# Causal mask of an attention's diagonal tile: a matmul with a mask, or an add on VectorE

## What is computed

```python
q = rotary_embedding(q, seq_len, HEAD_DIM)
k = rotary_embedding(k, seq_len, HEAD_DIM)
scores = jnp.einsum('bqhd,bkhd->bhqk', q, k) * scale
mask = jnp.tril(jnp.ones((seq_len, seq_len), dtype=bool))[None, None, :, :]
scores = jnp.where(mask, scores, NEG_INF)
weights = jax.nn.softmax(scores, axis=-1)
out = jnp.einsum('bhqk,bkhd->bqhd', weights, v)
```

## Time and profile before

| what | value |
|---|---|
| median of three runs | 2990.51 us |
| lowest, highest | 2986.48, 2994.03 us |
| profiled execution | 2990.0 us, of which 2988.3 us are the span of the program |
| busy share of the span: PE, DVE, ACT, POOL | 91%, 66%, 56%, 50% |
| granted TensorE clock, mean | 0.965 |

### The profile page before, as it was taken

How to read it: one execution, slowest core, us unless ns; L and a number is a source line. 1 busy time by engine, 2 the same in 40 slices (tenths; PEclk the granted TensorE clock), 3 DMA queues, 4 the chain that set the end, 5 groups by cost and what they waited for, 6 DMA issues and landing times. The chain is left out here.

```text
span 2988.3 us, 49627 instructions
## 1 busy us (share of the span) xinstructions
PE 2731.2 (91%) x15887; PEld 2292.6 (77%) x15887; DVE 1978.7 (66%) x3727; ACT 1663.8 (56%) x3193; POOL 1491.8 (50%) x1681
## 2 busy tenths in 40 slices
PE   5899989999989999899999689999959999999997
PEld 3788868888868888788888568778747888888886
DVE  5476766666756766566766669888845666666665
ACT  2456565656556656556666533333316676666665
POOL 1567555666646576546464434444423444444444
PEclk8999999999989999999999899999979999999999
DMA  3544443353534443433342555555433434444432
GB/s 123 106 115 106 105 117 91 91 128 87 123 87 108 101 120 92 122 90 89 91 102 62 155 154 153 142 142 143 125 129 67 99 81 99 99 99 99 99 56 49
DMA packets 193144, 316.79 MB, mean 106 GB/s; under 512 B 60896, under 2 KB 107008, under 8 KB 189888
## 3 DMA queue, kind: packets, MB, share of 16 engines
q1 hardware_dynamic: 147920, 214.94, 29.0%
q0 software_dynamic: 43952, 97.46, 13.3%
q10 hardware_dynamic: 1088, 2.11, 0.2%
HBM read 244.42 MB, written 75.17 MB: 107 GB/s over the span
## 5 line engine op out<-in xcount | busy, mean ns | idle before, releaser
L1026 ACT ACTIVATE a_pt<-a_PT 128x512 fp32r<-128x512 f32 (+3 forms) x768 | 350.4, 490 | 538.2 <-PE a_PT L891 537.4
L1100 DVE TENSOR_REDUCE a_nmax<-a_S 128x1 f32<-128x1024 f32 (+7 forms) x512 | 384.4, 751 | 273.3 <-PE a_S L880 272.0
L1109 DVE TENSOR_TENSOR a_pt<-a_PT,a_pt 128x512 fp32r<-128x512 f32 (+3 forms) x768 | 401.3, 549 | 191.4 <-ACT a_pt L1026 189.7
L908 PE MATMUL a_O<-a_pt,a_v 128*128 128x256 f32 (+1 forms) x2560 | 358.0, 287 | 49.2 <-DVE a_ot L1124 25.0
L1015 ACT ACTIVATE a_pb<-a_S,a_nmax 128x1024 f32<-128x1024 f32 (+7 forms) x512 | 380.3, 743 | 18.4 <-DVE a_nmax L1100 18.3
L908 PEld LDWEIGHTS a_O<-a_pt,a_v 128*128 128x128 f32 x2560 | 327.9, 194 | 64.4 <-DVE a_ot L1124 30.7
L891 PE MATMUL a_PT<-a_ident,a_pb 128*128 128x128 f32 x2304 | 342.6, 276 | 33.6 <-DVE a_pt L1109 32.3
L2068 DVE TENSOR_TENSOR e_w<-early_stage,e_w 128x1024 fp32r<-128x1024 f32 x238 | 280.8, 1219 | 121.5 <-ACT e_w L2018 121.4
L891 PEld LDWEIGHTS a_PT<-a_ident,a_pb 128*128 128x128 f32 x2304 | 270.9, 142 | 77.0 <-issue 28.5
L878 PE MATMUL a_S<-a_kh,a_qs 128*128 128x512 f32 (+3 forms) x768 | 285.8, 372 | 4.2 <-DMA a_kl<-a_rot 4.2
L828 PE MATMUL a_Z<-early_xT,early_wq 128*128 128x512 f32 x512 | 240.2, 469 | 44.1 <-issue 15.7
(11 more groups left out here) (296 smaller groups left out, 6995.2 us busy)
## 6 DMA issues: line engine op xcount, KB each, us to landing
a_qs<-a_rot SPq DMA_DIRECT2D x256, 128.0 KB, 2.3
a_kh<-a_rot SPq DMA_DIRECT2D x256, 128.0 KB, 2.3
a_kl<-a_rot SPq DMA_DIRECT2D x256, 128.0 KB, 2.3
e_rows<-scr_hs SPq DMA_DIRECT2D x40, 516.0 KB
scr_attT<-a_ot SPq DMA_DIRECT2D x256, 64.0 KB, 2.1
m_att<-scr_attT SPq DMA_DIRECT2D x32, 512.0 KB
m_rb<-scr_rinv SPq DMA_DIRECT2D x64, 256.0 KB
early_stage<-in_wqk POOLq DMA_DIRECT2D x31, 512.0 KB, 4.2
```

What stands on the lines that cost most here:

```text
L908: mm = pe.matmul(O[:, c0:2 * P], v2[:, n % 2, kt, h, :, :].rearrange("p a d -> p (a d)"), pt[j % 2][:, part, kt, c0:2 * P], start=kt == 0 ...
L1026: act.activation(pt[u % 2][:, 0, 4 * s:4 * s + m, (qt % 2) * P:(qt % 2 + 1) * P], PT[(k + s) % 2][:, 0:m * P].rearrange("p (k q) -> p k q" ...
L1100: dve.tensor_reduce(nmax[:, u % GU:u % GU + 1], S[u % 2][:, 0:cols], AXX, ALU.max, negate=True).then_inc(s_nb, 1)
L1109: dve.tensor_tensor(pt[u % 2][:, 1, 4 * s:4 * s + m, q], PT[(k + s) % 2][:, 0:m * P].rearrange("p (k q) -> p k q", k=m), pt[u % 2][:, 0, 4 ...
```

## The change

The 128x128 mask is kept once, in float32, and without the identity. TensorE's list loses L880 in each of the 512 tiles, and the last low product of the scores now ends the accumulation and raises `s_sfull`. VectorE's `rowmax` gains, ahead of the reduction, an add of the mask to the last 128 columns of S, in place in PSUM, and a wait for that add on a new semaphore, since the reduction reads what it wrote. GpSimd loses one memset and one affine_select at the start, and the wait for the constant moves from TensorE to VectorE. The order of everything else is the same on every engine.

```diff
-        identb = rm.sb("identb", [P, P], BF16)
-        maskb = rm.sb("maskb", [P, P], BF16)
+        mask = rm.sb("mask", [P, P])
...
+        s_masked = rm.sem("masked")
...
-            gp.memset(identb[:, :], 0.0).then_inc(s_pool, 1)
-            gp.memset(maskb[:, :], 0.0).then_inc(s_pool, 1)
+            gp.memset(mask[:, :], 0.0).then_inc(s_pool, 1)
...
-            gp.wait_ge(s_pool, 4)
-            gp.affine_select(out=identb[:, :], in_=identb[:, :], compare_op=ALU.not_equal, fill=1.0,
-                             base=0, pattern=[[-1, P]], channel_multiplier=1).then_inc(s_pool, 1)
-
-            gp.affine_select(out=maskb[:, :], in_=maskb[:, :], compare_op=ALU.is_ge, fill=MASKED,
+            gp.wait_ge(s_pool, 3)
+            gp.affine_select(out=mask[:, :], in_=mask[:, :], compare_op=ALU.is_ge, fill=MASKED,
...
-            pe.wait_ge(s_pool, 6)
...
                     pe.matmul(out, q, kh[:, sl, c0:c1], start=True, stop=False)
-                    pe.matmul(out, q, kl[:, sl, c0:c1], start=False, stop=c1 != cols)
-                pe.matmul(S[u % 2][:, cols - P:cols], identb[:, :], maskb[:, :],
-                          start=False, stop=True).then_inc(s_sfull, 1)
+                    mm = pe.matmul(out, q, kl[:, sl, c0:c1], start=False, stop=True)
+                mm.then_inc(s_sfull, 1)
...
             dve.wait_ge(s_tab, 2)
+            dve.wait_ge(s_pool, 4)
...
                 dve.wait_ge(s_sfull, u + 1)
+                last = S[u % 2][:, cols - P:cols]
+                dve.tensor_tensor(last, last, mask[:, :], ALU.add).then_inc(s_masked, 1)
+                dve.wait_ge(s_masked, u + 1)
                 dve.tensor_reduce(nmax[:, u % GU:u % GU + 1], S[u % 2][:, 0:cols], AXX, ALU.max,
                                   negate=True).then_inc(s_nb, 1)
```

## The result

| | before | after |
|---|---|---|
| median of the executions | 2988.49 us (4) | 3027.3 us (4, 3016.3 to 3030.88) |
| profiled execution | 2990.0 us | 3016.3 us |
| its span | 2988.3 us | 3014.5 us |

The ratio is 1.0122, with a 95% interval of 1.009 to 1.0155: the change costs 1.2%. The forecast was 3009 us with a range of 2984 to 3030, slower with a chance of 0.59.

The account below looks back on a forecast made before the run. TensorE, busy 91%, was taken as the fuller engine, but its waits for VectorE in attention decided where costs land. Terms summed to +18.5 us on the profiled 2990.0 us, giving 3008.5, or 3009 us as median; range 2984 to 3030.

Parts of the forecast that it names:

- What TensorE saves: Dropping L880 from TensorE's score products saves 0.12 us per tile, at most 61 us over 512 tiles.
- Pairs 6/7 and 14/15: Wide-plus-narrow tile steps, numbered modulo 16, where slack covers the add and TensorE's gain arrives: -0.24 us each, -14.9 us in all.
- What VectorE pays: Add plus the reduction's wait for it on VectorE: 0.28 + 0.04 = 0.32 us per tile, 164 us in all.
- The pairs led by VectorE: Steps 0/1, 2/3 and 10/11, where TensorE already waits for VectorE: +0.26 us at 93 places, +24.2 us.
- The cheap add: Rival: the wait costs nothing and each add on VectorE counts 0.20 us, so 2989 us, no change; chance 0.20.
- The eight kinds of pair: Wide-plus-narrow tile steps modulo 16, each booked separately: from +0.26 us to -0.24, with 4/5 at -0.04 (-1.2 us in all).
- The steps with statistics: Steps 6 to 9 with an input tile's statistics: VectorE leads, +0.64 us instead of -0.36 at 9 places, +9 us.
- The copies: VectorE's input-tile copies (L1087), for which TensorE's L908 waits: the add lies in the way, 24 x 0.32 = +7.7 us.
- 8/9 with 12/13: Step pairs where VectorE idles before L1109, so the add is hidden and half TensorE's saving arrives: 62 x -0.12 = -7.4 us.
- a dear add: Rival: VectorE's add costs the upper bound of 0.46 us, 23 us more; chance 0.19 together with VectorE falls behind.
- TensorE's gain arrives: Rival: TensorE's earlier signal pulls everything forward and the add fits VectorE's idle time: 2930 us, or 2960 for half; chance 0.11.
- VectorE falls behind: Rival: VectorE also leads steps 6 to 9 without statistics, some 20 more places, up to 3029 us; chance 0.19 with a dear add.

Follow-up runs that it names:

- with the product kept: Kernel before, its mask product on TensorE kept, plus an add of zeros with its wait on VectorE in the changed kernel's place: 3041.0 us, ratio 1.0173.
- the mix: Against the kernel before: mask product in pairs 0/1, 8/9 and every second group's step 7, elsewhere reduction first and add ahead of part_low: 2964.7 us, ratio 0.9926.
- the kernel with one more add: Like the mix, but step 7 has the late add ahead of part_low in every group of 16: 2972.2 us, ratio 0.9952 against the kernel before.

## Why the prediction was right, and where it was too small

*What TensorE saves (0.12 us each, 61 in all at most).* Right in size: a pair that waits for nobody gained 0.19 to 0.25 without a mask, so 0.10 to 0.12 for each product, and the matmul after the last low product follows at TensorE's pace again. Pairs 6/7 and 14/15 were booked at -0.24 and came at -0.21 and -0.19. And right that most is waited away: 26 us came. The sign "TensorE busy some 118 us less" failed: 40 us less, with 66 us more idle time instead of 80. The rows of L880 overlapped with their neighbours', as the forecast itself had said of their price.

*What VectorE pays (0.32).* It measured 0.33 at a wide tile: 0.30 + 0.03, against 0.28 + 0.04 (the mean of the adds is 0.293). An add in place in PSUM costs hardly more than the write to SBUF of the earlier trace rows. The pairs led by VectorE grew by 0.33 to 0.34 with the product kept. The cheap add, and with it the rule of the Trainium skill (VectorE: DVE Perf Modes, The DRAIN you can't avoid) that a semaphore after each instruction costs nothing extra, doesn't hold in this kernel, where the next instruction waits for it: the reduction starts 0.03 us behind the add's end, where an unwaited instruction starts 0.08 before it (893.17 + 1.09 = 894.26, then 894.18).

*Where it lands.* The eight kinds of pair came out within 0.05 us of the working, wherever neither a copy nor statistics nor a batch end is in them.

*The steps with statistics* were booked at +0.64 instead of -0.36. Measured: -0.21, and for 8/9 +0.67 where no copy lies beside them, thus +0.46. (At six of the nine places a copy does, and 8/9 is +0.94; the copy's part of it is counted below.) Right in kind, and 2 us too large in the sum.

*The copies are the step that failed.* "24 x 0.32": I took one copy for each of 24 input tiles, but a tile is copied in two halves, 48 copies in all, and each is awaited by a product of values. The earlier trace rows already had 33 such waits, more than 24. Every one of the 48 became a wait (48 times 0.82 us against 33 times 0.68 before). Against the same pairs without a copy, the 18 at 12/13 cost 0.33 each, the 9 at 0/1 0.33 (+0.60 instead of +0.27), the 6 at 4/5 0.60, and the 15 at 8/9 some 0.26. That is 16.4 us instead of 7.7. At 0/1 a copy has two adds in its way, that of step 0 and that of step 1; a pair 4/5 with a copy loses its slack as well.

*The sum.* With the measured medians put in, the first 31 groups give 27 us: 24.2 for the pairs led by VectorE, as booked; -8.1, -0.3 and -12.4 for 8/9 with 12/13, 4/5, and 6/7 with 14/15; 7.2 for the statistics; 16.4 for the copies. The traces agree (26.9). The batch ends, booked at +3, came to about nothing, and the last group took 1.5 us more instead of 1.9 less (5.7 more when the kernel ran again). So that 18.5 and the 8.7 of the copies come near the 26.3 of the span is in part luck: smaller errors cancel, and so do the 2.9 us that the later phases were shorter by.

*Memory and expert phases keep their times*: within 3 us (1289.3 and 1286.4 us). What the sum could not hold is the clock: the forecast went by one execution, and the changed kernel's executions spread over 14.6 us, those of before over some 10. The median, 3027.3 us, lies inside the range by 2.7 us only, and the upper bound had been set for a dear add or for VectorE falling behind, of which neither came: that the range held it is partly luck too.

*The rivals.* TensorE's gain arrives: no, the slack at L828 and L908 was nil, as argued. VectorE falls behind: not beyond the places named; in groups without statistics 8/9 is -0.13. It was the forecast's own mechanism with a larger count, and with executions slower than the first on top (at a lower clock, as far as the traces tell), that brought the median close to the time given for this rival.

## What to carry to other kernels

Before moving work from the busier engine to the less busy one, find where the first waits for the second, and count those places. Count them in the program, by the instructions that release, and hold the count against the waits in the trace. In this kernel an instruction ahead of a release cost its full length at each, while the engine relieved gained only in the stretches that wait for nobody. The place within the step decided more than the engine: the same change, an add for a product, cost 35 us with the add ahead of the releases, saved 9 with it behind them, and cost 113 with it at the end of the step, where it held up a third engine. And a way chosen for each pair from pairs measured one by one could be composed: the mix came out at its sum, though the kernel with one more add did not, because of what stood behind it in ScalarE's list.

## What the runs showed of the hardware that I had not expected

- VectorE adds in place in PSUM, 128 x 128 in float32, in 0.293 us on average (0.281 to 0.300), and the matmuls beside it keep their length, 349 ns.
- With TensorE's pauses some 5 us long at the batch ends, the same kernel's last tiles ran at 0.91 of the full clock in one execution and at 0.83 in another, and the last 92 us of the attention took 5 us longer.
- An instruction of VectorE that waits for the one before starts 0.03 to 0.04 us after its end, and one that doesn't wait starts 0.08 us before it (886.68 and 894.18 above, 609.71 in the earlier trace rows): a wait on itself costs about 0.11 us.
